# Four calls of the gather held back on GpSimd, and a new order of calls, in a fused ViT tower on one core

## The reference, cut to what matters

```python
h = einsum(patchify(x), tok_W) + tok_b                         # 196 tokens of 256 an image
# attention, on layernorm(h)
xn = x / max(norm(x), eps) * g
u, v, base = split(silu(xn @ uv_w.T))                          # 512, 512 and 128 wide
q, k = rope(base * gamma + beta)
kernel = square(relu((q @ k.T + w_rel[idx]) / sqrt(128)))
h = h + x * res_scale + (u * (kernel @ v)) @ o_w.T
# trees, on layernorm(h)
logits = x @ W_in.T + b_in                                     # 8 trees x 255 nodes
for d in range(7): current = child(current, logits[current] > 0)
out = (silu(logits) * visited_nodes) @ W_out.T                 # only the nodes on the path count
h = h + out
```

## Time and profile before

| | |
|---|---|
| median of the three runs | 2202.36 us (2202.06 to 2208.44) |
| span of the profiled execution, first to last instruction | 2199.5 us |
| TensorE busy | 2066.1 us, 94% |
| VectorE busy | 1621.5 us, 74% |
| ScalarE busy | 1395.2 us, 63% |
| GpSimd busy | 774.1 us, 35% |
| mean granted clock of TensorE | 0.981 of full speed |

### The profile page before, as it was taken

How to read it: one execution, slowest core, us unless ns; L and a number is a source line. 1 busy time by engine, 2 the same in 40 slices (tenths; PEclk the granted TensorE clock), 3 DMA queues, 4 the chain that set the end, 5 groups by cost and what they waited for, 6 DMA issues and landing times.

```text
span 2199.5 us, 42461 instructions
## 1 busy us (share of the span) xinstructions
PE 2066.1 (94%) x13256; PEld 1941.8 (88%) x13256; DVE 1621.5 (74%) x4210; ACT 1395.2 (63%) x3085; POOL 774.1 (35%) x905
## 2 busy tenths in 40 slices
PE   6899999999999999999999999999999999999997
PEld 5789889899988898888998898988889988889887
DVE  5678777777777787777777777777777877777775
ACT  5556666666666566566666665666665666656654
POOL 2752333232333333332323333323323233333233
PEclk8999999999999999999999999999999999999999
DMA  5331322222322223222223222222223232222222
GB/s 146 85 94 52 89 73 66 73 76 63 83 71 65 81 55 84 75 64 73 77 62 84 70 73 73 64 75 77 65 70 84 55 85 69 73 73 66 63 67 74
DMA packets 81999, 163.13 MB, mean 74 GB/s; under 512 B 17102, under 2 KB 48048, under 8 KB 81968
## 3 DMA queue, kind: packets, MB, share of 16 engines
q0 software_dynamic: 40960, 103.02, 17.4%
q1 hardware_dynamic: 41008, 59.71, 9.3%
HBM read 148.76 MB, written 13.90 MB: 74 GB/s over the span
## 4 chain that ended last, share of the span: by engine, by line
PE 84%; another core or an unknown queue 5%; ACT 4%; POOL 3%; issue 2%; DVE 1%; DMA 1%; ACTq 0%; POOLq 0%; SPq 0%; DVEq 0%
PE front L1142 10%; PE front L1144 9%; PE front L1143 9%; PE hid_ps L1142 9%; PE hid_ps L1143 9%; PE hid_ps L1144 9%; PE out_acc L1142 6%; PE out_acc L1143 6%; PE out_acc L1144 6%; PE out_acc L1378 4%; PE front L1177 2%; PE front L1184 2%; PE hid_ps L1366 2%; PE hid_ps L1337 2%
## 5 line engine op out<-in xcount | busy, mean ns | idle before, releaser
L474 POOL DMA_INDIRECT leaf_rows<-leaf_table,leaf_at x512 | 532.4, 1040 | 163.9 <-issue 163.4
L453 POOL TENSOR_TENSOR inv_root<-to_root,minus_half 98x8 f32<-98x8 f32 x64 | 111.0, 1734 | 728.3 <-DVE to_root L885 404.6
L528 ACT ACTIVATE hid_hi<-hid 128x392 fp32r<-128x392 f32 (+1 forms) x256 | 177.8, 695 | 237.1 <-PE out_acc L1144 155.4
L1142 PE MATMUL out_acc<-hid_hi,outw_lo 128*128 128x392 f32 x768 | 293.4, 382 | 2.6 <-DVE hid_lo L835 2.3
L1142 PE MATMUL hid_ps<-ffn_x,in_lo 128*128 128x392 f32 x768 | 282.3, 368 | 6.2 <-POOL in_lo L445 5.8
L1143 PE MATMUL hid_ps<-ffn_x,in_hi 128*128 128x392 f32 x768 | 266.3, 347 | 0.0
L1144 PE MATMUL hid_ps<-ffn_x,in_hi 128*128 128x392 f32 x768 | 264.7, 345 | 0.0
L1144 PE MATMUL out_acc<-hid_hi,outw_hi 128*128 128x392 f32 x768 | 264.6, 345 | 0.0
L1143 PE MATMUL out_acc<-hid_lo,outw_hi 128*128 128x392 f32 x768 | 264.4, 344 | 0.0
L473 POOL TENSOR_TENSOR held<-minus_half 98x1 f32<-98x1 f32 x128 | 47.2, 369 | 489.9 <-issue 428.7
L718 ACT ACTIVATE leaf_rows<-leaf_rows,leaf_act 98x256 f32<-98x256 f32 x512 | 218.2, 508 | 0.1
(11 more groups left out here) (140 smaller groups left out, 5808.2 us busy)
## 6 DMA issues: line engine op xcount, KB each, us to landing
x_raw<-x SPq DMA_DIRECT2D x192, 196.0 KB, 2.4
out<-out_stage SPq DMA_DIRECT2D x32, 392.0 KB
leaf_rows<-leaf_table,leaf_at POOLq DMA_INDIRECT x512
leaf_table<-leaf_rows SPq DMA_DIRECT2D x4, 256.5 KB, 4.7
out_stage<-in_w SPq DMA_DIRECT2D x4, 256.0 KB
tok_major<-tok_w SPq DMA_DIRECT2D x3, 256.0 KB, 4.3
late_raw<-out_w SPq DMA_DIRECT2D x6, 128.0 KB
u<-uv_w SPq DMA_DIRECT2D x1, 576.0 KB, 4.2
```

The source lines that it names most:

```text
L453: pool.tensor_tensor(inv_root[:, 0:size], to_root[:, 0:size], minus_half[:, 0:size], ALU.pow).then_inc(roots_ok, 1)
L474: pool.indirect_dma_start(row_slot(s, g), None, table, bass.IndirectOffsetOnAxis(ap=leaf_at[:, s, g:g + 1], axis=0), element_offset=s * P ...
L528: act.activation(out, src, ACT.Copy).then_inc(done, 1)
L1142: pe.matmul(out, w[1], x_parts[0], start=start, stop=False)
```

## The change

GpSimd's `fetch_rows` gets a further argument. The second tree's first call now waits until `v_ok` shows that unit n's first v group has its silu. In each body the calls of the first, second and fourth tree fetch group 2 before group 1, and the late splits of the first unit stand between whole runs of four. The lists of calls of the other three engines are written in a new order, with the same calls in them.

```diff
-            def fetch_rows(i, s, g):
+            def fetch_rows(i, s, g, n=None):
 
                 if i is None:
                     return
+                if g == 0 and n is not None:
+                    pool.wait_ge(v_ok, GROUPS * n + 1)
                 if g == 0:
...
                 fetch_rows(i, 0, 0)
+                fetch_rows(i, 0, 2)
                 fetch_rows(i, 0, 1)
-                fetch_rows(i, 0, 2)
                 fetch_rows(i, 0, 3)
-                fetch_rows(i, 1, 0)
                 late_splits(i, n, 2)
+                fetch_rows(i, 1, 0, n)
+                fetch_rows(i, 1, 2)
                 fetch_rows(i, 1, 1)
...
                 silu_base(n)
+                silu_v(n, 0)
                 scale_base(n, 1)
-                scale_base(n, 0)
                 leaf_silu(i, 0)
-                silu_v(n, 0)
...
                 make_base(n)
+                make_v(n, 0)
                 tree_logits(i, 4, 1)
-                make_v(n, 0)
+                tree_out(i, 2, 0)
                 make_v(n, 1)
```

More of the change, by code:

```diff
@@ L784, in body @@
-                if first(n):
-                    build_rows()
                 kern_high(n, 0)
@@ L1052, in body @@
                 norm_stats(n, 0, 1)
+                norm_moments(n, 0)
                 decisions(i, 0)
-                norm_moments(n, 0)
+                decisions(i, 1)
+                mask(i, 0)
                 hid_low(p, 7)
-                mask(i, 0)
-                decisions(i, 1)
-                hid_low(i, 0)
                 decisions(i, 2)
                 mask(i, 1)
+                if first(n):
+                    build_toward()
+                hid_low(i, 0)
                 decisions(i, 3)
@@ L1068, in body @@
                 residual(n, 1)
+                hid_low(i, 2)
+                leaf_dots(i, 0)
+                rotate_qk(n, 1)
                 decisions(i, 4)
[L1070 removed]
                 mask(i, 3)
[L1072 to L1073 removed]
+                v_low(n, 0)
+                decisions(i, 5)
+                v_low(n, 1)
                 rotate_qk(n, 0)
[L1075 to L1076 removed]
+                v_low(n, 2)
                 qk_low(n, 0)
                 qk_low(n, 1)
+                hid_low(i, 3)
                 leaf_dots(i, 1)
[L1080 to L1083 removed]
                 mask(i, 4)
+                v_low(n, 3)
                 add_rel_bias(n, 0)
+                add_rel_bias(n, 1)
                 square_relu(n, 0)
[L1087 to L1088 removed]
                 square_relu(n, 1)
@@ L1091, in body @@
                 kern_low(n, 1)
-                decisions(i, 5)
-                decisions(i, 6)
-                hid_low(i, 4)
-                gate(n, 0)
-                leaf_dots(i, 2)
-                gate(n, 1)
-                mix_low(n, 0)
+                x_low(nx, 0)
+                hid_low(i, 4)
+                mask(i, 5)
+                gate(n, 0)
+                mix_low(n, 0)
+                gate(n, 1)
+                decisions(i, 6)
                 gate(n, 2)
@@ L1102, in body @@
                 gate(n, 3)
-                mask(i, 5)
+                hid_low(i, 5)
                 mix_low(n, 3)
-                x_low(nx, 0)
                 x_low(nx, 1)
+                leaf_dots(i, 2)
+                x_low(nx, 2)
                 mask(i, 6)
@@ L1417, in body @@
                 project_o(i, 1, range(0, EC))
+                tree_logits(p, 7, 0)
                 embed(n, 0)
@@ L1420, in body @@
                 turn_h(i, 1, 1)
-                tree_out(p, 4, 1)
                 embed(n, 1)
-                tree_logits(p, 7, 0)
                 tree_logits(p, 7, 1)
                 embed(n, 2)
+                tree_out(p, 5, 0)
                 embed(n, 3)
@@ L1428, in body @@
                 embed(n, 5)
-                add_rows(p, 2)
                 turn_ffn_x(i, 0)
                 turn_ffn_x(i, 1)
-                tree_out(p, 5, 0)
+                tree_out(p, 5, 1)
                 tree_visits(p, 7)
-                tree_out(p, 5, 1)
+                add_rows(p, 2)
                 turn_h(n, 0, 0)
                 turn_h(n, 0, 1)
+                tree_out(p, 6, 0)
                 tree_logits(i, 0, 0)
-                tree_out(p, 6, 0)
+                tree_logits(i, 1, 0)
+                if first(n):
+                    turn_rows()
+                tree_visits(i, 0)
                 tree_out(p, 6, 1)
-                tree_visits(i, 0)
-                tree_logits(i, 1, 0)
                 tree_logits(i, 2, 0)
```

131 lines of the change are left out of this document (59 added, 72 removed).

## The result

| | before | after |
|---|---|---|
| median (range) | 2202.21 us (2200.37 to 2208.44), 4 runs | 2078.35 us (2077.75 to 2079.96), 4 runs |
| profiled execution: span | 2199.5 us | 2075.9 us |
| its own time | not given | 2077.75 us |
| mean granted clock | 0.981 | 0.993 |

The ratio is 0.943, with a 95% interval of 0.9415 to 0.9444: 124 us faster. The forecast was 2117 us, with a range of 2086 to 2180. Later sets of runs then showed what no view of the first two profiles can: the whole gain is there on some chips and absent on others.

A forecast was written before the change was run, and what follows sets the result against it. TensorE was taken as the bound, idle 94.7 us through its late signals during GpSimd's fetches. Terms -73 - 16 + 6 - 2 = -85 took the span from 2199.5 to 2114.5; plus 2.9 carried over, 2117 us, range 2086 to 2180.

The forecast's parts named there:

- What bounds the kernel, and where: TensorE sets the time; its 94.7 us idle ahead of `make_base` and `make_v` come from its late signals while GpSimd fetches.
- The split, -73 us: Holding back the second tree's four fetches removes most idle ahead of `make_base` and `make_v`, leaving 0.7 us per unit.
- The clock, -16 us: Most falls of TensorE's granted clock behind the stall should not come; three quarters of 21 us taken.
- The order of calls: New call order puts TensorE's products over the three silus and `silu_v(0)` before the scalings; no gain put on it.
- What the wait queues, +6 us: Later fetches and `norm_roots` stand behind GpSimd's added wait; 0.2 us per unit lost.
- The start, -2 us: In the first unit a fetch now stands behind a late-weight split TensorE waits for; at most 2.6 us gained.
- half the idle left and no clock gain: Slow end of the forecast's own range, given as 2157 us.
- runs meet again: Rival, chance 0.12: second and third fetch runs join to eight beside `make_u` and `scores`, half the gain gone, 2160 us.
- the rows come too late: Rival, chance 0.08: VectorE's `leaf_dots(1)` waits 3.5 us per unit for fetched rows, 109 us, giving 2226 us.
- the one for one of the prediction: All of VectorE's 3.5 us wait for rows counted on the path, 31 x 3.5 = 109 us.
- the 2.7 us per unit: Size of VectorE's wait for late rows from which that rival was to decide against the 85 us won.
- the rival that drew on this rule (0.06): The split does nothing, chance 0.06: lateness comes from something else or the rule holds; 2202 us, give or take the order.

The follow-up runs named there:

- set 5: Runs on one chip: kernel before unchanged 2063.61 us, changed kernel unchanged 2070.86 us, changed kernel with plain transfers in place of gathers 2063.48 us.
- first pair: The study's first measurement and profiles of the kernel before and the changed kernel: 2202.21 us against 2078.35 us.
- set 4: Runs on one chip: kernel before unchanged 2205.51 us, changed kernel unchanged 2076.65 us; two further variants 2271.65 and 2076.77 us.
- split alone: Kernel before with only GpSimd's part of the change (added wait, whole runs of four, late splits between them), other engines' calls in old order: 2156.92 us, ratio 0.9795.
- set 3: Runs on another chip (kernel before 2061.78 us); the one meant: changed kernel, second tree's fetches held until `add_rows(0)`, joining second and third run: 2239.88 us, ratio 1.0856.
- joined run: Changed kernel without the added wait, ScalarE's `leaf_number(i, 1)` moved earlier, so the first two runs join to eight: 2276.62 us, ratio 1.0302; again 2271.65 us.
- sets 1, 2 and 4: Runs on three different chips, where the kernel before took 2201.87, 2208.51 and 2206.83 us.
- order alone: Changed kernel without the added wait, new order of calls on all engines: 2093.26 us, ratio 0.9496.

## Why the prediction was right or wrong

**What bounds the kernel, and where: right.** TensorE's idle time lay in one place, it came from late signals, and with the second run held back it is gone (94.7 us to 1.7).

**The split, -73 us: the step that failed.** Two things in it were wrong, both to the low side. *"With nothing late, all 94.7 us of idle go"* was set as the bound, and it is none. The clean kernel before of set 5 gives the true price, start to start. From the second turn to `make_base` it takes 0.37 us, in the earlier trace rows 1.79; from there to `make_v(0)` 2.30 against 3.58; from there to `make_v(1)` 1.37 against 2.41. The differences are 1.42 + 1.28 + 1.04 = 3.74 us per unit, of which the profile records 2.98 as idle. One reason stood ahead of the prediction: a matmul's end is modelled. Products follow each other every 0.18 us and are drawn 0.34 long, so at each of the three stalls the drawn tail covers some 0.16 us of the gap, about 0.5 of the missing 0.76; the rest isn't accounted for. 31 x 3.74 = 116 us. (A whole undisturbed unit is 66.45 us against 62.46, 3.99, so a little more is lost outside these three steps.) *"0.7 us left per unit"* was the second: the pace of the changed kernel is 63.03 us in the first pair (62.92 in set 4) and 62.79 where no signal is late, so 0.24 at most is left, 7 us. The term was -109, where the prediction had -73.

**The clock, -16 us: mis-sized.** In the changed kernel's loop no fall of the granted clock is left, so all of it came back, about 21 us by the prediction's own working.

**The order of calls, no gain put on it: wrong twice.** On a chip where nothing is late, order and wait together cost 0.27 us per unit (62.79 less 62.52), 8 us: that is set 5's 0.4%. I put it to the order, though the two weren't timed apart there. On a chip with late signals it is what makes the split worth having: the split alone brought 45 us, with the order 124. I had checked each call for what it might gain and not for what the wait needs from it: `silu_v(0)` early enough that the second run neither meets the third nor comes late for `leaf_dots(1)`.

**What the wait queues, +6 us: nothing.** 1.66 us lie between second and third run, and TensorE is full at 63.03 of 63.03 us.

**The start, -2 us: wrong in sign, and small.** TensorE's waits for the late weights (`in_lo`) are 6.9 us in the changed kernel and were 5.8.

With the sizes put right: -109 - 21 + 8 + 1 = -121, against the -123.6 of the spans. One slip in the prediction changes nothing: half the idle left and no clock gain gives 2155 us (2202.4 less 47.35), not 2157.

**The rivals.** That runs meet again, and that the rows come too late, both happened in the split alone, and the order kept both off. The late rows had the right mechanism: TensorE stood 52.2 us in all behind them. Their price was fair to a little low: in set 3 144.5 us of waiting for them cost 170 us, more than the one for one of the prediction, with clock falls behind TensorE's stalls (mean granted clock 0.969, against 0.991 with the rows in time). But the 2.7 us per unit from which they were to outweigh the gain don't hold as a wait of VectorE's: in the split alone it stood 115.7 / 31 = 3.7 us per unit, and the kernel was still 45 us faster than before. The meeting runs brought few late signals there (31 of 349 changes), so that their price of 43 us was not tested by itself. A joined run beside `make_base` in the new order, of which the prediction had no term, costs 195 us.

**The rule of the Trainium skill** (SBUF — State Buffer, "SBUF: two separate sides"), by which a DMA can't slow a compute operation, agrees with the chips of sets 3 and 5. There the kernel before has a pace of 62.52 us with gathers, and a steady unit of 62.46, and TensorE never stands for them. On the chips of sets 1, 2 and 4 the durations obey it too (0.34 us a product beside the fetches, as elsewhere), but the signals behind them do not. Had the first pair been timed on a chip of the second kind, the change would have been worth nothing, as the rival that drew on this rule (0.06) said: 2070.86 us against 2062.38. That the forecast had the right sign is owed in part to the chip that it was timed on.

What makes the signals late, and why on some chips only, is open. Shown are: not the bytes alone, not the store; gathers and not plain transfers of the same bytes; TensorE's signals and no other engine's; no lateness at all on two of the five chips of the experiments. Within a set all runs of the kernel before agreed within 1%, so it isn't something that comes and goes between executions. But each chip was used in one set only, so a trait of the chip isn't told apart from one of its machine or of that session; "kind of chip" stands for any of these. Of the versions that compute the reference, none beats the changed kernel on the first kind of chip, and none beats the kernel before on the second.

## What to carry to other kernels

Price a stall of TensorE from start to start against an undisturbed stretch, not from the recorded idle time, which missed a fifth of it here. When a run of gathers on GpSimd is cut in two, look at three distances at once: from its end to the products whose signals matter, from the second part to the next run, and from its landing to whoever reads the rows; the wait alone brought 45 of 124 us, and the new order with a joined run lost 68. And if a cost hangs on "remote" releases of one's own engines, time the kernel on more than one chip before it is tuned around.

## What the runs showed of the hardware that was not expected

- TensorE's signals, and no other engine's, late by up to 4.8 us in the timelines beside a run of eight gathers on three chips, and by nothing on two, with the same program, the same fetches and the same durations: 2202 to 2209 us against 2062.
- A gap of 1.16 us in a run of eight gathers was enough to save the silu of the base (order alone); in the one unit with a gap of 0.42 us TensorE stood 3.4 us.
- Four plain transfers from GpSimd's queue took 2.3 us where four gathers of the same bytes took 5.
- Over 8 us that take in a stall of 4.4 us TensorE's mean granted clock was 0.61, most of it at its lower level of 1.2 GHz (new order with the joined run; 0.955 over its whole span, against 0.981 of the kernel before, whose stall came in three steps of about 1 us).
